# 16-head cross-attention on one Trainium2 core: scores made twice from stacked high and low operands, and P no longer transposed

## What is computed

```
Q = (layernorm(x) @ wq.T + bq) in 16 heads of 8;  K, V from ctx in the same way
scores = Q . K / sqrt(8);  scores = where(mask == 0, -1e-09, scores)
x = x + (softmax(scores) . V) @ wo.T + bo
```

## Time and profile before

| | |
|---|---|
| median of 3 runs | 1812.39 us (1811.54 to 1815.43) |
| the profiled execution: its own time | 1815.55 us |
| the profiled execution: span | 1813.7 us, mean granted PE clock 0.849 |
| busy in the span | PE 1415.0, PEld 1061.2, DVE 1143.6, ACT 616.5, POOL 265.5 us |
| `mha` of layer 0, 2, 3 stands at | 34 to 237, 988 to 1163, 1588 to 1764 us |
| `prep_mha` of layer 0, 3 stands at | 16 to 33, 1579 to 1588 us |

### The profile page before, as it was taken

How to read it: one execution, slowest core, us unless ns; L and a number is a source line. 1 busy time by engine, 2 the same in 40 slices (tenths; PEclk the granted TensorE clock), 3 DMA queues, 4 the chain that set the end, 5 groups by cost and what they waited for, 6 DMA issues and landing times. The chain is left out here.

```text
span 1813.7 us, 26829 instructions
## 1 busy us (share of the span) xinstructions
PE 1415.0 (78%) x7716; PEld 1061.2 (59%) x7749; DVE 1143.6 (63%) x3741; ACT 616.5 (34%) x1055; POOL 265.5 (15%) x237
## 2 busy tenths in 40 slices
PE   3999976999976663302760999699999999789982
PEld 1666665998964453201540777567777777557761
DVE  5777774576647875670243888645556655578868
ACT  1444403444433220000110555334444444345541
POOL 1222100010101100064246222000000000032202
PEclk8999986999995555555875999799999999989995
DMA  6000000000000031002321000000000000000001
GB/s 218 1 0 0 0 1 1 1 2 0 1 1 1 0 124 30 0 20 84 113 69 32 1 0 0 1 1 1 1 1 0 0 0 1 1 1 0 0 1 47
DMA packets 38579, 34.21 MB, mean 19 GB/s; under 512 B 8672, under 2 KB 35552, under 8 KB 38112
## 3 DMA queue, kind: packets, MB, share of 16 engines
q1 hardware_dynamic: 35168, 26.78, 4.9%
q0 software_dynamic: 3328, 6.43, 1.1%
HBM read 24.15 MB, written 9.44 MB: 19 GB/s over the span
## 5 line engine op out<-in xcount | busy, mean ns | idle before, releaser
L392 PE MATMUL mha_pS<-mha_kbd,mha_qT 128*128 128x512 f32 x384 | 203.9, 616 | 3.6 <-ACT mha_qT L450 3.4
L484 POOL TENSOR_TENSOR mha_kbd<-KT,w_ctx 128x1024 f32<-128x1024 f32 x48 | 91.2, 1901 | 758.3 <-SPq L97 460.5
L1982 DVE SCALAR_TENSOR_TENSOR tree_hl<-tree_pH,tree_hh 128x512 fp32r<-128x512 f32 x192 | 132.4, 689 | 94.8 <-ACT tree_hh L1879 93.2
L425 PEld LDWEIGHTS mha_pO<-VB,mha_PT 128*128 128x128 f32 x1536 | 183.2, 192 | 10.8 <-issue 8.7
L425 PE MATMUL mha_pO<-VB,mha_PT 128*128 (+1 forms) x1536 | 178.3, 259 | 0.0
L1879 ACT ACTIVATE tree_hh<-tree_pH 128x512 fp32r<-128x512 f32 x192 | 114.6, 597 | 146.1 <-PE tree_pH L1783 112.1
L518 DVE TENSOR_REDUCE mha_nm<-mha_pS 128x8 f32<-128x512 f32 x192 | 131.6, 686 | 44.4 <-PE mha_pS L396 24.1
L521 DVE TENSOR_TENSOR mha_Z<-mha_pS,mha_nm 128x512 f32<-128x512 f32 x192 | 132.9, 692 | 19.3
L462 ACT ACTIVATE mha_PT<-mha_pT 128x1024 f32<-128x1024 f32 x96 | 98.3, 1024 | 136.5 <-PE mha_pT L407 136.0
L457 ACT ACTIVATE mha_PR<-mha_Z 128x1024 f32<-128x1024 f32 x96 | 101.5, 1057 | 86.1 <-DVE mha_Z L521 86.0
L407 PEld LDWEIGHTS mha_pT<-w_ctx,mha_PR 128*128 128x128 f32 x768 | 87.4, 141 | 38.4 <-issue 38.2
(11 more groups left out here) (422 smaller groups left out, 2822.8 us busy)
## 6 DMA issues: line engine op xcount, KB each, us to landing
w_tree_full<-in_tree_full_dram SPq DMA_DIRECT2D x1, 4224.0 KB, 14.2
exp_W<-in_L_W_dram SPq DMA_DIRECT2D x32, 128.0 KB, 2.3
slots_in<-route_zero SPq DMA_DIRECT2D x40, 64.0 KB, 1.8
w_rot<-in_rot_dram SPq DMA_DIRECT2D x1, 2307.0 KB, 8.7
X<-in_x_dram SPq DMA_DIRECT2D x8, 256.0 KB, 5.8
exp_xe<-slots_in SPq DMA_DIRECT2D x16, 128.0 KB, 3.0
slots_out<-exp_ye POOLq DMA_DIRECT2D x16, 128.0 KB, 2.9
out_dram<-X SPq DMA_DIRECT2D x8, 256.0 KB, 2.3
```

Source lines behind the costliest of these rows:

```text
L392: ins = pe.matmul(pS[:, n, :], qT[u][:, P * v:P * v + P], kbd[u][:, 8 * n:8 * n + 8, :], start=True, stop=not key_mask)
L425: ins = pe.matmul(pOv[:, c, :], PT[v][:, P * c:P * c + P], VB[:, a.b(-2), c, :], start=True, stop=True)
L484: pool.tensor_tensor(kbd[u][:], kb, bmask.unsqueeze(2).to_broadcast([P, H, SK]), ALU.mult).then_inc(s["kbd"], 1)
L1982: dve.scalar_tensor_tensor(hl[k % 2][:], pH[k % 2][:], 0.0, hh[k % 2][:], ALU.max, ALU.subtract).then_inc(s["lo"], 1)
```

## The change

Queries and keys are split in a high part rounded to the format of the fast matmul (float32r, one pass) and the rest. `wk3` holds the weights of the keys three times over, so that one product of `prep_parts` gives 96 rows: the keys of four heads (32 rows), as high, low, high; `KS` holds these for the four groups of heads. The queries go through the same form by DMA: `qh`, `qh`, `ql` to the three sets of 32 rows of `qs`. A product over 96 rows then gives high x high + high x low + low x high. Scores are made twice, both in float32r: once as tokens x keys (`pS`, L412), only to find each head's maximum, and once as keys x tokens (`pST`, L433), with eight more rows through which the negative maximum, in two parts, is added in the product itself. That one goes through exp straight to `PT`, ready as the stationary operand of the product with the values. For it the maxima are split (`nx`, DVE L577, L579), transposed (PE L422), copied (`nT`, ACT L498) and sent to the rows of `qs` by four DMAs for each batch (L378).

- Gone: `Z` and its subtraction, `PR`, the eight transposes of P, the copy to `PT`, the bfloat16 products of layer 0, the separate normalisation on DVE (ACT does it now, L481, one tile at a time) and a copy of the statistics.
- Queries are made for four tiles at once (`QT = 4`), 12 DMAs each time (L372). `pS` and `pST` have one buffer each, of two PSUM banks; `pN`, which takes the transposed maxima, shares its bank with `pA`, and `heads_T` waits for `nT` for that reason.
- A step of a tile now stands further behind its scores: transposed scores 3 slots, the product with the values 5, output 6, the sum to X 7. The slots run from -7 to 39 and are all written out, where a loop stood before.
- `prep_parts` makes the keys in eight products with two buffers in turn, each read by ACT and then by DVE.
- The stage of layer 0 starts with three memsets of 3 x 2048 on DVE (rows of ones).
- The routing stage now stands ahead of the allocation of layer 2's buffers, which moves no instruction.

The core of the diff:

```diff
+        if key_mask:
+            pe.wait_ge(s_c, 1)
         for n in range(2):
-            pe.matmul(pk[n], w("wk"), c2[:, 8 * n:8 * n + 8, 0, :], start=True, stop=True).then_inc(s_k, 1)
+            ctx = kc[:, 8 * n:8 * n + 8, :] if key_mask else c2[:, 8 * n:8 * n + 8, 0, :]
+            for g in range(NQ):
+                need(pe, s_l, NQ * n + g - 1)
+                pe.matmul(pk[g % 2][0:3 * HR, :], w("wk3")[:, 3 * HR * g:3 * HR * g + 3 * HR], ctx, start=True, stop=True).then_inc(s_k, 1)
         for b in range(B):
...
+        dve.memset(KS[3 * HR:last, :, :].bitcast(F32), 1.0).then_inc(s_z, 1)
...
+        lo = slice(HR, 2 * HR)
+        for n in range(2):
+            for g in range(NQ):
+                dve.wait_ge(s_kt, NQ * n + g + 1)
+                kl = KS[lo, g, 512 * n:512 * n + 512]
+                dve.scalar_tensor_tensor(kl, pk[g % 2][lo, :], w("bk3")[lo, g:g + 1], kl, ALU.add, ALU.subtract).then_inc(s_l, 1)
...
+        pS = st.ps("pS", [P, H, SK])
+        pST = st.ps("pST", [P, CU, S])
+        pQ, pO, pAb, pYb = (st.ps(n, [P, 512]) for n in ("pQ", "pO", "pA", "pY"))
...
+            def queries(q, groups):
+                u = q % QB
+                if groups[0] == 0:
+                    sp.wait_ge(s["q"], q + 1)
+                    need(sp, s["ST"], QT * (q - QB) + QT)
+                for g in groups:
+                    r = slice(HR * g, HR * g + HR)
+                    for n, src in enumerate((qh, qh, ql)):
+                        sp.dma_start(plain(qs[u][HR * n:HR * n + HR, g, :]), plain(src[r, :])).then_inc(s_ld[u], 16)
+            def shifts(b):
+                u, c0 = (b // 2) % QB, S * (b % 2)
+                sp.wait_ge(s["nT"], b + 1)
+                for g in range(NQ):
+                    sp.dma_start(plain(qs[u][K0:K1, g, c0:c0 + S]), plain(nT[b % 2][2 * NH * g:2 * NH * g + 2 * NH, :])).then_inc(s_m[b % 2], 16)
...
+            for t in range(FIRST, LAST):
+                if t % QT == 0 and live(t + 4):
+                    queries(quad(t + 4), (0, 1))
+                if t % QT == 1 and live(t + 3):
+                    queries(quad(t + 3), (2, 3))
+                if not even(t) and live(t - 1):
+                    shifts((t - 1) // TB)
...
+            def scores(t):
+                b, q = t // TB, quad(t)
+                u, c0 = q % QB, P * (t % QT)
+                if t % QT == 0:
+                    pe.wait_ge(s_ld[u], LD * (q // QB + 1))
+                if even(t):
+                    pe.wait_ge(s["k"], b + 1)
+                need(pe, s["nm"], t)
+                for g in range(NQ):
...
+                for g in range(NQ):
+                    ins = pe.matmul(pS[:, NH * g:NH * g + NH, :], qs[u][0:KC, g, c0:c0 + P], ks[b % KB][0:KC, g, :, :],
+                                    start=True, stop=True)
...
+            def shifts(b):
+                pe.wait_ge(s["nx"], b + 1)
+                need(pe, s["aT"], TB * b - 4)
+                need(pe, s["nT"], b)
+                for v in range(TB):
+                    src = nx[b % 2][:, v, :, :, :].rearrange("p g n h -> p (g n h)").bitcast(F32)
+                    ins = pe.transpose(pN[:, P * v:P * v + P], src, ident)
+                ins.then_inc(s["nTp"], 1)
...
+            def scores_T(b, i):
+                u, c0 = (b // 2) % QB, S * (b % 2)
+                if i == 0:
+                    pe.wait_ge(s_m[b % 2], LM * (b // 2 + 1))
+                need(pe, s["P"], TB * b + i)
+                for n in range(CU):
+                    c = CU * i + n
+                    g, h0 = c // 2, 2 * (c % 2)
+                    ins = pe.matmul(pST[:, n, :], ks[b % KB][0:K1, g, h0:h0 + 2, :], qs[u][0:K1, g, c0:c0 + S], start=True, stop=True)
+                ins.then_inc(s["ST"], 1)
+            def attend(t):
+                b, v = divmod(t, TB)
+                pe.wait_ge(s["P"], TB * b + 2)
+                need(pe, s["at"], t)
+                for c in range(CH):
+                    ins = pe.matmul(pOv[:, c, :], PT[b % PB][:, c, P * v:P * v + P], VB[:, b, c, :], start=True, stop=True)
+                ins.then_inc(s["O"], 1)
+            def heads_T(t):
+                pe.wait_ge(s["at"], t + 1)
+                need(pe, s["aT"], t)
+                need(pe, s["nT"], min(B, (t + 6) // TB))
+                pe.transpose(pA, at[t % 2][:], ident).then_inc(s["aTp"], 1)
+            def output(t):
+                pe.wait_ge(s["aT"], t + 1)
+                need(pe, s["X"], t)
+                pe.matmul(pY, aT[t % 2][:], w("wo"), start=True, stop=True).then_inc(s["Y"], 1)
...
+            for t in range(FIRST, LAST):
+                if live(t):
+                    scores(t)
+                if live(t - 6):
+                    heads_T(t - 6)
+                if live(t - 5):
+                    attend(t - 5)
+                if live(t - 6):
+                    output(t - 6)
+                if live(t - 3):
+                    b = (t - 3) // TB
+                    scores_T(b, t - 3 - TB * b)
+                if not even(t) and live(t - 1):
+                    shifts((t - 1) // TB)
+                if t % QT == 2 and live(t + 6):
+                    x_transposes(quad(t + 6))
+                if t % QT == 3 and live(t + 5):
+                    queries(quad(t + 5))
...
+            def shifts(b):
+                act.wait_ge(s["nTp"], b + 1)
+                if b >= 2:
+                    act.wait_ge(s_m[b % 2], LM * (b // 2))
+                act.activation(nT[b % 2][:], pN, ACT.Copy).then_inc(s["nT"], 1)
+            def exponentials(b, i):
+                n = TB * b + i
+                act.wait_ge(s["ST"], n + 1)
+                if mask is not None:
+                    act.wait_ge(s["G"], n + 1)
+                need(act, s["O"], TB * (b - PB) + 2)
+                act.activation(PT[b % PB][:, CU * i:CU * i + CU, :], pST[:], ACT.Exp, scale=SC).then_inc(s["P"], 1)
...
+            for t in range(FIRST, LAST):
+                if live(t - 6):
+                    heads_T(t - 6)
+                if live(t + 9) and t + 9 >= QT:
+                    normalise(t + 9)
+                if live(t - 3):
+                    b = (t - 3) // TB
+                    exponentials(b, t - 3 - TB * b)
+                if not even(t) and live(t - 1):
+                    shifts((t - 1) // TB)
+                if t % QT == 2 and live(t + 6):
+                    x_evac(quad(t + 6))
+                if t % QT == 3 and live(t + 5):
+                    q_evac(quad(t + 5))
...
+                need(pool, s["ST"], TB * (b - KB) + 2)
+                kb = KS[0:K1, :, SK * b:SK * b + SK].unsqueeze(2).to_broadcast([K1, NQ, NH, SK])
+                hb = heads[0:K1, :].unsqueeze(1).unsqueeze(3).to_broadcast([K1, NQ, NH, SK])
+                pool.tensor_tensor(ks[b % KB][0:K1, :, :, :], kb, hb, ALU.mult).then_inc(s["k"], 1)
...
+                def q_low(q):
+                    dve.wait_ge(s["qh"], q + 1)
+                    dve.scalar_tensor_tensor(ql[:], pQ[:], w("bq"), qh[:], ALU.add, ALU.subtract).then_inc(s["q"], 1)
+                def largest(t):
+                    b, v = divmod(t, TB)
+                    dve.wait_ge(s["S"], t + 1)
+                    top = nm[b % 2][:, v, :]
+                    if not masked:
+                        dve.tensor_reduce(top, pS[:], AX.X, ALU.max, negate=True).then_inc(s["nm"], 1)
...
+                def split_shift(b):
+                    dve.wait_ge(s["nm"], TB * b + 2)
+                    need(dve, s["nTp"], b - 1)
+                    src = nm[b % 2][:].rearrange("p v (g h) -> p v g h", h=NH)
+                    dve.tensor_copy(nx[b % 2][:, :, :, 0, :], src).then_inc(s["nh"], 1)
+                    dve.wait_ge(s["nh"], b + 1)
+                    dve.tensor_tensor(nx[b % 2][:, :, :, 1, :], src, nx[b % 2][:, :, :, 0, :], ALU.subtract).then_inc(s["nx"], 1)
...
+                for t in range(FIRST, LAST):
+                    if live(t):
+                        largest(t)
+                    if live(t - 7):
+                        r = t - 7
+                        dve.wait_ge(s["Y"], r + 1)
+                        dve.wait_ge(s["bo"], r // TB + 1)
+                        dve.tensor_tensor(X[:, r, :], pY, X[:, r, :], ALU.add).then_inc(s["X"], 1)
+                    if live(t) and not even(t):
+                        split_shift(t // TB)
+                    if live(t - 7):
+                        dve.wait_ge(s["X"], r + 1)
+                        dve.bn_stats(bn[r % 2][:], X[:, r, :]).then_inc(s["bn"], 1)
+                    if live(t - 5):
+                        dve.wait_ge(s["O"], t - 4)
+                        dve.reciprocal(rc[(t - 5) % 2][:], pOv[:, :, 2 * HD:VW]).then_inc(s["rc"], 1)
+                        need(dve, s["aTp"], t - 6)
+                        dve.wait_ge(s["rc"], t - 4)
+                        dve.tensor_tensor(at[(t - 5) % 2][:].rearrange("p (c h d) -> p c h d", h=2, d=HD),
```

More of the change, by code:

```diff
@@ L26 @@
 VW = 2 * HD + 2
+HR = P // 4
+NH, NQ = H // 4, 4
 EPS = 1e-5
```

(19 more changed lines are left out.)

376 lines of the change are left out of this document (145 added, 231 removed).

## The result

The changed kernel took 2018.99 us (median of 4 runs, 2006.82 to 2038.04), the kernel before 1813.91; the ratio is 1.110, 95% interval 1.107 to 1.113. The ratio leaves out the slow run of the four, 2038.04, which lies 1.6% above the fastest. It is slower by 11%, where 1808 was forecast within 1784 to 1842. The profiled execution took 2006.82 us, its span is 2005.1, 191.4 over the 1813.7 of before.

The account below looks back on a forecast made before the run. PE's own work was taken to bound the old kernel, waits around exp the new loop. Stages save 32.3 us, preparations cost 27.5, so -4.8 from 1812.4 gives 1808 us, range 1784 to 1842.

Parts of the forecast that it names:

- the seventh distance between tiles: Of a stage's 31 distances, the first six at the low clock take 23.4 us; then nineteen at 4.31 follow.
- the loop: Steady tiles of a stage: value products and exp wait for each other; four tiles 17.24 us, 4.31 a tile against 5.04.
- the drain: End of each attention stage: seven slots in which the chain still runs, 24.0 us.
- the clock falls: Rival: PE's short idles in the loop lower its clock; 5.64 a tile, 1915 us if throughout; chance 0.07.
- PE's 3.7: PE's own work for a tile after the change, 3.7 us against 5.04, if PE stayed the bound.
- The row of the trees' drain: Evidence cited against a falling clock: it kept 1.00 there with PE in flight 2.54 of 4 us.
- The first two rivals: Loop: shorter handovers, 1771 us, chance 0.13; short float32r products not hiding their loads, 1857 us, chance 0.18.
- the change of rows: PE's products in a tile: 0.2 us once where the number of rows changes, bounds none to 0.4.
- the opening sum of a tile before: PE's work for one tile of the old loop, 4.94 us summed against 5.04 in the timeline.
- The preparation: Making keys and values before the stages: layer 0 +14 us, layer 3 +13.5, layer 2's hidden under gather waits.
- The fill: Stage start between scale part and loop: queries made and sent by twelve DMAs, 14.4 us against 3.6 before.
- The sum: All stages and preparations together: -32.3 + 27.5 = -4.8 us, so 1808; main case chance 0.62.

Follow-up runs that it names:

- r2_before_narrower: Kernel before, P's transposes replaced by 18-column float32 products, in layers 2 and 3 also a tile's second 512-column score product; 2092.38 us, ratio 1.151.
- e3_pad_small: Changed kernel with three extra float32 products of 18 columns per slot behind the scores, where PE waits for exp; 2069.76 us, ratio 1.140.
- g1_mix: Changed kernel with value products 144 columns wide for the first 8 tiles and from tile 25, 72 in between; 1815.51 us, 1.000 of before.

## Why the prediction was wrong

- **The step that failed is the clock.** The low clock was counted for the start of a stage alone; from the seventh distance between tiles on, every term of the loop and of the drain was counted at 1.00, by the earlier trace rows, and "the clock falls" had a chance of 0.07. The argument against it was that at the lower level PE would be without idle time and that such work had brought the clock up before. PE was without idle time, and it didn't: 19.8 of 20 us in flight at 0.50 here, 20.00 of 20 in `r2_before_narrower`. I took a busy PE for one whose clock comes up. A row with PE in flight all the time says nothing of the mix of its work, and the change removes the widest products; with 144 columns in the value products and nothing else changed, the clock is back at 1.00 and 191 us are gone.
- **The rival that came true was mispriced.** 1915 was its time. Its 5.64 a tile is 1.94 over PE's 3.7, which is about what everything but the 1.71 of the value products costs: I took these at nearly the same price at both levels, since they move few columns. They went from 1.71 to 3.28. So 5.64 a tile became 6.37, with short stretches at the full clock in it, and a stage 238 to 241 us instead of 204.
- **Its mechanism was wrong too.** The Trainium skill ("TensorE: Matmul & The Clock Gate", on cycling through PSUM) puts such a swing down to short idles between groups. Here the runs disagree: with 144 columns PE idles a fifth of a stretch in the middle of layer 3 at 1.00 (6.36 of 8 us in flight), and filling the idle time with narrow products leaves 0.59 (`e3_pad_small`). The row of the trees' drain had pointed the same way.
- **The loop was right.** With the clock at 1.00, four tiles take 17.20 us against 17.24 (with 72 columns, 0.13 a tile dearer than the 1.71 I had taken, so that the rest was as much cheaper), and PE's waits are those for exp and `nT`. The first two rivals fell: the handovers are not shorter, and the float32r products cost 0.14 each (1.12 a tile for all eight, 1.16 forecast with the change of rows), not 0.22. A wait that I hadn't in the chain is that of the product with `wo` for the sum to X (0.4 at most with 144 columns, 0.6 with 72, behind DVE's low part). One slip changes nothing: the opening sum of a tile before, given as 4.94, leaves out the 0.11 of the transposes of x; with them it is 5.05, against 5.04.
- **Around the loop.** The preparation in layer 0 took +14.6 (+14 forecast) and in layer 3 +14.4 (+13.5), and layer 2's stayed hidden as forecast. The three memsets of layer 0 took 6.1 and not 5.3 (48.28 to 54.35). The fill was 1.0 longer: first scores 19.3 us after the start (1036.56 to 1055.82), 18.3 forecast. SP issued a DMA each 0.63 us and not 0.48 (1046.85 to 1053.79 for eleven distances), and the scores came 2.03 after the twelfth was issued, which bounds its landing; 2.1 was taken. The page of the kernel after has 2.0 for the landing, and 64 KB for each of these DMAs, where the prediction gives 8 to 16. The Trainium skill ("DMA: Bandwidth & Descriptors", on the anatomy of a transfer) states the fit that the prediction cites for DMAs that GpSimd issues, and these are SP's; the 2.15 us worked out from it is an estimate beside the 2.0 measured.
- **The sum** of -4.8 us, 0.997 of before, was a little too good apart from the clock: `g1_mix`, the same kernel with the clock kept, measures 1.000 (0.998 to 1.001), some of it for its wider products. That it comes so near is in part luck. In its profiled execution each stage is longer than forecast (174.2 in layers 2 and 3 against 172.2, 180.3 in layer 0 with its memsets against 177.5), and the part between layers 0 and 2 is 5.5 shorter than before the change (744.8 against 750.3), which nothing in the forecast gives.
